# Dense work of four layers of a graph network, moved from between the gather passes into them

## The reference, cut to what matters

```
rgcn:  sums = segment_sum(x[src], dst * 10 + edge_type); mean = sums / max(cnt, 1)
       out  = einsum('nrd,rdo->no', mean, w_rel) + x @ root + bias          (twice, 10 relations)
rel:   msg  = (feature @ weight[rel])[rel, src] * norm; segment_sum(msg, dst) (3 relations)
sage:  agg  = segment_sum(h[src], dst) / deg; agg @ Wl.T + bl + h @ Wr.T     (twice, then batch norm, fc)
filter: segment_sum(h[src] * W(edge), dst)
```

## Time and profile before

| | before |
|---|---|
| median of 3 runs | 18150.66 us (18142.34 to 18160.76) |
| profiled execution, its time | 18060.58 us |
| its span | 18058.9 us |
| POOL busy | 10776.4 us (60%) |
| PE busy | 8078.5 us (45%) |
| DVE busy | 6968.1 us (39%) |
| ACT busy | 3051.7 us (17%) |

### The profile page before, as it was taken

One profiled execution on the slowest core, in us unless ns is written; L12 is line 12 of the kernel. 1 busy time (PEld: TensorE's weight loads), 2 busy tenths in 40 slices (PEclk: granted clock), 3 DMA queues, 4 the chain that ended last, 5 costly groups with the idle time before them and its releaser, 6 DMA issues.

```text
span 18058.9 us, 179436 instructions
## 1 busy us (share of the span) xinstructions
PE 8078.5 (45%) x36107; PEld 6392.7 (35%) x36108; DVE 6968.1 (39%) x28429; ACT 3051.7 (17%) x6469; POOL 10776.4 (60%) x10307
## 2 busy tenths in 40 slices
PE   2463333362222243333343333433233477777777
PEld 1233333332222233333333333322222355555555
DVE  7632222234444442222232222244444434444443
ACT  0132222220000020000020000100000144444443
POOL 0046666636666636666646666566666358888882
PEclk6575555585555575555565555555555567777775
DMA  2143333341111131111121111133333256666665
GB/s 89 53 162 89 88 88 87 84 161 45 45 44 44 44 100 45 46 45 45 47 65 45 45 45 45 50 86 85 85 86 86 72 102 119 118 118 118 118 118 122
DMA packets 1043036, 1436.88 MB, mean 80 GB/s; under 512 B 208285, under 2 KB 644148, under 8 KB 1042956
## 3 DMA queue, kind: packets, MB, share of 16 engines
q0 software_dynamic: 552016, 851.84, 21.7%
q1 hardware_dynamic: 490984, 584.65, 11.2%
HBM read 1101.27 MB, written 334.40 MB: 79 GB/s over the span
## 4 chain that ended last, share of the span: by engine, by line
another core or an unknown queue 29%; issue 21%; DVE 21%; DMA 10%; PE 6%; POOL 6%; ACT 3%; DVEq 2%; ACTq 0%; POOLq 0%; SPq 0%
DMA agg_dram<-acc,sum_row 8%; DVE tab_s L1215 5%; DVE scratch L1215 5%; POOL agg_dram L619 5%; DVE xn_h L1223 3%; DVE xs L1185 3%; DVE acc L1171 2%; PE ps L1010 2%; PE ps L968 1%; DVE tab_s L1157 1%; DMA table_dram<-tab_s 1%; ACT yT L670 1%; DVEq L345 1%; PE ps L967 1%
## 5 line engine op out<-in xcount | busy, mean ns | idle before, releaser
L633 POOL DMA_INDIRECT rows<-table_dram,row_st x4160 | 3970.3, 954 | 2199.8 <-issue 1251.5
L633 POOL DMA_INDIRECT scratch<-table_dram,row_st x4160 | 3970.2, 954 | 2175.7 <-issue 1257.9
L840 PE MATMUL ps<-scratch 128*128 128x128 f32 x8320 | 2012.5, 412 | 3843.6 <-DMA scratch<-table_dram,row_st 1313.3
L840 PE MATMUL ps<-tab_s,rows 128*128 128x128 f32 x8320 | 1997.9, 410 | 3793.5 <-DMA rows<-table_dram,row_st 1420.1
L840 PEld LDWEIGHTS ps<-scratch 128*128 128x128 f32 x8320 | 1753.3, 307 | 4083.9 <-issue 2865.6
L840 PEld LDWEIGHTS ps<-tab_s,rows 128*128 128x128 f32 x8320 | 1745.1, 306 | 4026.8 <-issue 2894.4
L619 POOL DMA_INDIRECT agg_dram<-acc,sum_row x1664 | 2633.3, 1583 | 529.1 <-issue 392.5
L1171 DVE TENSOR_TENSOR acc<-ps,acc 128x128 f32 x2080 | 607.8, 292 | 4859.3 <-remote 4294.5
L692 ACT ACTIVATE row_st<-row_i 128x16 int32 (+1 forms) x520 | 111.4, 214 | 9994.8 <-remote 8056.3
L1215 DVE TENSOR_SCALAR scratch<-ps,rw_st 128x128 f32<-128x128 f32 x3328 | 1126.9, 402 | 406.9 <-issue 370.7
L1215 DVE TENSOR_SCALAR tab_s<-ps,rw_st 128x128 f32<-128x128 f32 x3328 | 1124.0, 401 | 309.4 <-issue 280.6
(11 more groups left out here) (193 smaller groups left out, 10968.3 us busy)
## 6 DMA issues: line engine op xcount, KB each, us to landing
scratch<-in_src_row SPq DMA_DIRECT2D x832, 256.0 KB
table_dram<-tab_s POOLq DMA_DIRECT2D x200, 640.0 KB, 3.2
scratch<-type_dram SPq DMA_DIRECT2D x416, 256.0 KB
scratch<-in_dst_row SPq DMA_DIRECT2D x416, 256.0 KB
rows<-table_dram,row_st POOLq DMA_INDIRECT x4160
scratch<-table_dram,row_st POOLq DMA_INDIRECT x4160
scratch<-table_dram SPq DMA_DIRECT2D x416, 64.0 KB
agg_dram<-acc,sum_row POOLq DMA_INDIRECT x1664
```

The lines of the kernel that those rows point to most:

```text
L633: pool.indirect_dma_start(row_banks[bank][:, u, :], None, table_dram[p["rels"]], bass.IndirectOffsetOnAxis(ap=row_st[:, bank, u:u + 1], ax ...
L840: mm = pe.matmul(ps[bank][:, q * P:(q + 1) * P], rows[:, u, :], hot[:, u, :], start=u % QUAD == 0, stop=u % QUAD == QUAD - 1)
```

## The change

The layers 1 to 4 (`FLOWS`) are taken apart. 23 of the 25 superblocks (`in_pass`) of layer k now run inside gather pass k, the pass whose sums they read. `walk` gets a form that goes in blocks of four groups; in block b the superblock b - 3 is worked on, in four steps kk = 0 to 3 that stand in each engine's order behind the group's own work. The last two superblocks run in a `tail` behind the pass. Each layer has a table of its own, since the gathers of pass k still read table k - 1 while table k is being written. ACT copies all chunks; SP issues the stores. The chunks of a superblock in the pass use one PSUM bank in layers 1 and 2 and two in layers 3 and 4. `acc` is set by `flow_keep` and, with a root product, `flow_init`. A check on the chip compares each tile's first destination with what the lag needs, and takes the general path where it doesn't hold.

```diff
+BLOCK = 4
+LAG = 3
+FLOWS = (1, 2, 3, 4)
...
+    nblocks = ngroups // BLOCK
+    in_pass = max(min(nblocks - LAG, nsb - 2), 0)
...
+        ROOT = {1: 6, 3: 2, 4: 2}
+        BANKS = {1: [6], 2: [6], 3: [6, 3], 4: [6, 3]}
...
+            def block(b, f):
+                for kk in range(BLOCK):
+                    g = b * BLOCK + kk
+                    body(g, kk % 2, b * 2 + kk // 2, isinstance(g, int) and g == 0, isinstance(g, int) and g == ngroups - 1,
+                         None if f is None else (f, kk))
+            if flow and in_pass:
+                block(0, None)
+                with e.Fori(0, LAG - 1) as i:
+                    block(i + 1, None)
+                ends = LAG + in_pass == nblocks and ngroups == nblocks * BLOCK
+                if in_pass - ends:
+                    with e.Fori(0, in_pass - ends) as f:
+                        block(f + LAG, f)
+                if ends:
+                    block(nblocks - 1, in_pass - 1)
+                for g in range((LAG + in_pass) * BLOCK, ngroups):
+                    body(g, g % 2, g // 2, False, g == ngroups - 1, None)
+                return
...
+            def flow_store(k, f, t, c):
+                p = DENSE[k]
+                table = table_dram[k].rearrange("(s j p r) c -> p s j (r c)", j=4, p=P, r=p["rels"])
+                j, (a, b) = c // len(cuts(p)), cuts(p)[c % len(cuts(p))]
+                sp.wait_ge(c_evac, chunks_so_far(reps, k, t) + (c + 5))
+                settle(sp)
+                sp.dma_start(table[:, bass.ds(f, 1), j, a:b].rearrange("p s w -> p (s w)"), out_st[k][c % 4][:, 0:b - a]
+                             ).then_inc(c_out[c % 4], 16)
...
+            def flow_y(k, f, t, adds):
+                p = DENSE[k]
+                act.wait_ge(add_done, adds)
+                if has_upd(p):
+                    act.wait_ge(s_upd, so_far(reps, k, has_upd, t) + 1)
...
+            def flow_norm(k, t):
+                n = so_far(reps, k, has_ln, t)
+                act.wait_ge(s_var, n + 1)
+                act.activation(nrm[:, :, 1], nrm[:, :, 0], ACT.Sqrt).then_inc(s_sd, 1)
+                act.wait_ge(s_nrm, n + 1)
+                act.wait_ge(s_hT_mm, n + 1)
+                for j in range(4):
+                    a = act.activation(h[:, j, :], xn[:, j, :], ACT.Relu, bias=nrm[:, j, 3:4], scale=nrm[:, j, 2:3])
+                a.then_inc(s_h, 1)
...
+            def flow_evac(k, t, c, banks):
+                p = DENSE[k]
+                a, b = cuts(p)[c % len(cuts(p))]
+                act.wait_ge(c_mm, chunks_so_far(reps, k, t) + (c + 2))
+                act.wait_ge(c_out[c % 4], chunks_so_far(reps, k, t) * 4 + (16 * (c // 4) + 16))
+                act.activation(out_st[k][c % 4][:, 0:b - a], ps[banks[c % len(banks)]][:, 0:b - a], ACT.Copy
+                               ).then_inc(c_evac, 1)
+            def flow_step(k, r, f, kk):
+                t = act.snap(r * in_pass + f)
+                if kk == 0:
+                    flow_y(k, f, t, adds_before(reps, k, r, f))
+                if has_ln(DENSE[k]):
+                    if kk == 1:
+                        flow_norm(k, t)
+                    if kk == 2:
+                        flow_hT(k, t)
+                    here = range(4) if kk == 3 else ()
+                else:
+                    here = range(4 * (kk - 1), min(4 * kk, n_chunks(DENSE[k]))) if kk else ()
+                for c in here:
+                    flow_evac(k, t, c, BANKS[k])
...
+            def flow_turn(k, t):
+                pe.wait_ge(s_h, so_far(reps, k, has_ln, t) + 2)
+                pe.wait_ge(s_hT, so_far(reps, k, has_ln, t) + 1)
+                for j in range(4):
+                    mm = pe.matmul(ps[5][:, j * P:(j + 1) * P], h[:, j, :], ident[:], start=True, stop=True)
+                mm.then_inc(s_hT_mm, 1)
...
+            def flow_chunk(k, t, c, banks):
+                p = DENSE[k]
+                j, (a, b) = c // len(cuts(p)), cuts(p)[c % len(cuts(p))]
+                source = flow_source(k, t) if c == 0 else hT_s if has_ln(p) else yT
+                if c == 0 and has_root(p):
+                    pe.wait_ge(s_init, so_far(reps, k, has_root, t) + 1)
+                pe.wait_ge(c_evac, chunks_so_far(reps, k, t) + (c - len(banks) + 5))
+                pe.matmul(ps[banks[c % len(banks)]][:, 0:b - a], source[:, j * P:(j + 1) * P], W[p["table"]][:, a:b],
+                          start=True, stop=True).then_inc(c_mm, 1)
+            def flow_step(k, r, f, kk, q):
+                p = DENSE[k]
+                if has_ln(p):
+                    if (kk, q) not in ((0, 0), (1, 1), (2, 0), (2, 1), (2, 2), (2, 3)):
+                        return
+                    t = pe.snap(r * in_pass + f)
+                    if kk == 0:
+                        flow_update(k, t)
+                    elif kk == 1:
+                        flow_turn(k, t)
+                    else:
+                        if q == 0 and has_root(p):
+                            flow_root(k, t, ROOT[k], BANKS[k])
+                        flow_chunk(k, t, q, BANKS[k])
+                elif kk * 4 + q < n_chunks(p):
+                    t = pe.snap(r * in_pass + f)
+                    flow_chunk(k, t, kk * 4 + q, BANKS[k])
+                    if kk * 4 + q == n_chunks(p) - 1:
+                        flow_root(k, t, ROOT[k], BANKS[k])
...
+                    if q == 3:
+                        mm.then_inc(group_mm, 1)
+                    if at is not None:
+                        flow_step(pn, r, *at, q)
...
+            dve.wait_ge(lag_made, (checked > 0) + (checked < ntiles))
+            step(dve.tensor_tensor(rel_dst[:], first_i[:], row_i[:], ALU.subtract))
+            step(dve.tensor_reduce(reps_f[:, 2:3], rel_dst[:], AX.X, ALU.min))
+            step(dve.tensor_scalar(reps_f[:, 2:3], reps_f[:, 2:3], -0.5, None, ALU.is_lt))
+            step(dve.tensor_tensor(reps_f[:, 0:1], reps_f[:, 0:1], reps_f[:, 2:3], ALU.add))
...
+                dve.tensor_scalar(acc_f, acc_f, keep, bias_once, ALU.mult, ALU.add).then_inc(s_keep, 1)
...
+                dve.scalar_tensor_tensor(out=acc_f, in0=ps[bank][:], scalar=once, in1=acc_f, op0=ALU.mult, op1=ALU.add
+                                         ).then_inc(s_init, 1)
...
+            def flow_x(k, t):
+                n = so_far(reps, k, has_ln, t)
+                dve.wait_ge(s_x_in, so_far(reps, k, has_x, t) * 16 + 16)
+                dve.wait_ge(s_x_out, so_far(reps, k, has_xout, t) * 16 + 16)
+                dve.wait_ge(s_h, n + 1)
+                dve.wait_ge(s_upd, so_far(reps, k, has_upd, t) + 2)
+                settle(dve)
+                dve.tensor_tensor(flat(xn), ps[4][:], flat(xs), ALU.add).then_inc(s_x_new, 1)
+                dve.wait_ge(s_x_new, so_far(reps, k, has_x, t) + 2)
...
+                dve.wait_ge(s_mv, n * 4 + 4)
+                dve.tensor_scalar(nrm[:, :, 0], mv[:, :, 1], EPS, None, ALU.add).then_inc(s_var, 1)
+                dve.wait_ge(s_sd, n + 1)
+                dve.reciprocal(nrm[:, :, 2], nrm[:, :, 1]).then_inc(s_rstd, 1)
...
+                adds = dve.snap(adds_before(reps, k, r, f) + 4 * (kk + last))
+                if kk == 1:
+                    if has_ln(DENSE[k]):
+                        flow_x(k, t)
+                    flow_keep(k, f, t, adds)
+                if kk == 3 and has_root(DENSE[k]):
+                    flow_init(k, f, t, ROOT[k], adds)
...
-                        dve.memset(acc[:], 0.0)
```

More of the change, by code:

```diff
@@ L74, in turns @@
     def turns(k, flag):
-        return nsb * sum(bool(flag(p)) for p in DENSE[:k])
+        return nsb * sum(bool(flag(p)) for j, p in enumerate(DENSE[:k]) if j not in FLOWS)
     def has_src(p): return p["src"] != ""
@@ L324, in build @@
         bn_ready = sem("bn_ready")
+        lag_made = sem("lag_made")
+        once_step = sem("once_step")
+        s_y = sem("s_y")
+        s_upd = sem("s_upd")
+        s_x_in = sem("s_x_in")
+        s_x_out = sem("s_x_out")
+        s_x_new = sem("s_x_new")
+        s_st = sem("s_st")
+        s_mv = sem("s_mv")
+        s_var = sem("s_var")
+        s_sd = sem("s_sd")
+        s_rstd = sem("s_rstd")
+        s_nrm = sem("s_nrm")
+        s_h = sem("s_h")
+        s_hT_mm = sem("s_hT_mm")
+        s_hT = sem("s_hT")
+        s_root = sem("s_root")
+        s_keep = sem("s_keep")
+        s_init = sem("s_init")
+        c_mm = sem("c_mm")
+        c_evac = sem("c_evac")
+        c_out = [sem(f"c_out{n}") for n in range(4)]
         settled = sem("settled")
@@ L401, in lane_uses @@
         def lane_uses(k, v):
-            return 1 + nsb * sum((4 // LANES if is_wide(p) else v == 0) for p in DENSE[:k] if has_table(p))
+            return 1 + nsb * sum((4 // LANES if is_wide(p) else v == 0) for j, p in enumerate(DENSE[:k])
+                                 if has_table(p) and j not in FLOWS)
         def wait_lane(e, k, i, j):
@@ L492, in _, with load_types @@
                     with sp.Fori(0, reps) as r:
```

(9 more changed lines are left out.)

281 lines of the change are left out of this document (238 added, 43 removed).

## The result

The changed kernel takes 18,689.56 us (18,681.12 to 18,734.38, four runs), the kernel before 18,155.71 beside it: ratio 1.030, 95% interval 1.028 to 1.032. It is slower by 3.0%. The forecast was 18,830. The profiled execution has a span of 18,679.4 us, 620.5 more than before.

A forecast was written before the change was run, and what follows sets the result against it. It took POOL's pauses between gathers, prolonged by late PE signals, to bound the kernel: 18150.7 us, less 699 for shorter gaps, plus 1380 for grown pauses, gives 18,830 us; range 18,300 to 19,000, chance 0.42.

The forecast's parts named there:

- The gaps: Dense layers between and behind gather passes: 879.7 us shrink to 176 (46, 55, 46, 29), so 704 us gone.
- The total: Whole kernel: net gain of 699 us against 1380 us of added pauses in four passes, forecast 18,830 us.
- That pauses, not busy time, decide: Gather passes: other engines have room for the moved work; POOL's pauses of 3.0 to 3.7 us a group set the length.
- Late signals of PE: Gather passes: a PE signal made inside an uninterrupted run of gathers arrives late, 21.6 us in one case.
- The first rival: Handshakes in the passes stay hidden, so the change is faster: 17,452 to 17,737 us, likeliest 17,550; chance 0.32.
- Pass 1, 28 us a block: 12 chunks on one bank: three to four chunk, copy and quad round trips in three groups' pauses, 35 us less 7.
- SP's added stores: SP's queue in the passes: 92 x (4 to 12) stores and x loads, all early and on its own queue.
- The norm chain, 6.2 us a block in passes 2 and 3: Adds, statistics and normalization ahead of staging group 2 grow that pause from 6.3 to 12.5 us.
- The pause added in half of the blocks: Pass 3: group 1's signal is late, so POOL stops after 16 gathers instead of 32, another 6.3 us.
- The chunks' round trips, 10 us in pass 2 and 3 in passes 3 and 4: Chunks wait for copies of earlier chunks: 10.5 us a block in pass 2, 3 in passes 3 and 4.
- Pass 2 as a whole: All added pause time in pass 2: 6.2 + 10.5 = 17 us a block, taken as 16.
- The walk's rule for signals: Walking through a block: PE's signal inside a run of gathers is late until the run breaks; in a pause, prompt.

The follow-up runs named there:

- e11: The kernel of e5 again, on a chip with late signals: 18,351.12 us, ratio 1.016.
- e5: The changed kernel with SP loading the next group's types before storing chunks in pass 1, on a chip without late signals: ratio 0.957.
- e2: The changed kernel; in pass 1 ACT and SP take the next group's relations and types before this group's copies and stores: 17,939.13 us, ratio 0.9934.
- e10: The kernel of e8 (relations ahead, norm behind staging, more banks) again, on a chip with late signals: 17,766.80 us, ratio 0.9778.
- e12: The kernel of e6 (relations ahead, norm behind staging, the change's banks) again, on a chip with late signals: 17,757.24 us, ratio 0.9821.
- e1: Only layers 3 and 4 moved into their passes, layers 1 and 2 as in the kernel before: 18,006.05 us, ratio 0.9965.
- e7: e2's kernel with three PSUM banks for chunks in layer 2 and four in layers 3 and 4, chip without late signals: ratio 0.957.
- e4: The kernel before plus a 1024-column POOL instruction behind the 8th gather of every group: 17,992.70 us, ratio 0.9962.
- e9: The changed kernel again, without an edit, on a chip of the slower kind: 18,748.79 us, ratio 1.031.
- e8: e2's kernel with both the edits of e6 and e7, on the chip without late signals: ratio 0.957.
- e6: e2's kernel with normalization behind the next group's staging in layers 2 and 3, transposes and chunks later, chip without late signals: ratio 0.957.

## Why the prediction was right, and where not

*The gaps.* Right to 2 us in 702, step by step: the fixed parts and two superblocks each.

*The total.* The cost of 1302 us is near 1380 by luck: by pass the forecast was 334 us too low, then 142, 194 and 77 too high.

*That pauses, not busy time, decide.* Right. The busy times of the engines fit in every variant, and the length of a pass followed the pauses alone.

*Late signals of PE as what makes the moved handshakes cost.* Shown by one kernel on two chips: its four passes take 10,714 us where signals are late (e11) and 8373 where they are not (e5), 4 x 2093 us of gathers. The changed kernel itself did not run on the second chip; e5 differs from it in SP's order alone. The first rival is what happens there: with no pause grown it gave 699 us of gain, 702 were measured in e5.

*Pass 1, 28 us a block.* This step failed in its mechanism: it counted round trips of chunk, copy and quad. It measured 42.5 (978 / 23), and of these some 19 are SP's type load behind the stores (the changed kernel to e11), 18 the relations behind ACT's copies (e2, on top of SP's order), and 5 all the rest, the round trips among them. These steps compare traces of different chips; pass 1 of e2, e10 and e12, on three chips, agrees within 36 us. A late signal was only the first link. What it released was a chain of loads and one-hots that the edit had put behind it in two in-order queues. The prediction named SP's added stores and called them early and alone on their queue; this was the wrong sentence.

*The norm chain, 6.2 us a block in passes 2 and 3.* The size was right, the place was taken for granted. The prediction let the pause before group 2 grow from 6.3 to 12.5 us, and in e1 it is 12.7. It is paid only where a pause falls before group 2: in pass 3 of the changed kernel none does, and with the normalization behind the staging the pauses there are 6.4 (e10, e12). The pause added in half of the blocks did not come: the runs of 32 stayed. In pass 2 the chain is worth 7.5 us a block (e11 to e12).

*The chunks' round trips, 10 us in pass 2 and 3 in passes 3 and 4.* Not seen at that size: no gain from more banks in pass 2, 1.5 us at most in pass 3, none in pass 4. More banks without the later normalization ran only on the chip without late signals (e7). Pass 2 as a whole measured 9.8 us a block for 16, pass 3 3.6 for 12, pass 4 0.7 for 4. These terms were too large; that and the missing 14.5 us of pass 1 cancelled in the sum.

*The walk's rule for signals*, late inside a run and prompt in a pause, was too simple: e4 made signals prompt inside runs. And the walk took one place of the pauses for all blocks. The cost of a pass follows from the groups before which its pauses fall. Pass 3 takes 2561 us when they are 0 and 2 (e1) and 2474 to 2483 when they are 1 and 3 (the changed kernel, e2, e11). Pass 4 takes 2415 to 2417 with 0 and 2 (the changed kernel, e9, e10), 2464 to 2465 with 1 and 3, in all blocks or all but one or two (e1, e11, e12; 8.9 and 6.4 us), and 2437 in e2, which has both. What decides between them was not found, so a forecast of such a pass has an uncertainty of 50 to 90 us.

*Open:* why signals of PE, and at times of DVE, are late at all. It is not the program, since e5 and e11 are the same. The ends of matmuls in a trace are estimates, so it is not shown whether PE's results are late or only its signals; in e5 all updates of `group_mm` in pass 3 come 0.01 us after these ends. Only e4 changed the lateness (34 of 102 updates of `group_mm` in pass 3 over 1 us late, before 53 of 94), and it did not remove it.

The best kernels are e10 and e12, 2.2% and 1.8% faster than the kernel before where signals are late; both were 4.3% faster where they are not (e8, e6).

## What to carry to other kernels

When work is moved into a loop whose bound engine waits for a staging instruction, list what then stands behind each new wait in every in-order queue that feeds the staging (here ACT and SP), and put the feeding work of the next round ahead of the new one; that was worth 854 us here, more than the gaps gained. Price a handshake by how long its signal takes in that stretch of the trace, not by the instructions. Look before which step of the loop the pauses fall: a chain costs only where one falls on it. And time such a change on more than one chip: one kernel (e5, e11) is 4.3% faster on one and 1.6% slower on another.
